# A graph attention and expert kernel on one core: TensorE runs a step's tail ends first, then tail weights, weighted sum and logits, and both folds together behind them

## What is computed

```python
x = x + L0_gnn(layernorm(x), adj, W, a)      # 8192 nodes, 256 features
x = x + L0_ffn(layernorm(x), ...)            # router over 32 experts, top 1

def L0_gnn(h, adj, W, a):
    Wh = h @ W
    e = (Wh @ a1)[:, None] + (Wh @ a2)[None, :]
    e = where(e > 0, e, 0.2 * e)
    e = where(adj > 0, e, -9e15)             # adj: 8192 x 8192 int32, about 4 ones in a row
    return elu(softmax(e, axis=1) @ Wh)

def L0_ffn(xf):
    idx = argmax(xf @ router_w.T + router_b)
    h = relu(xf @ W1[idx] + b1[idx])
    return relu(h @ W2[idx] + b2[idx])
```

## Time and profile before

| | before |
|---|---|
| time, median of 3 runs | 1303.84 us (1300.76 to 1303.9) |
| the profiled execution's own time | 1299.63 us |
| its span, from first to last instruction | 1297.9 us |
| busy: PE, DVE, ACT, POOL | 891.5, 886.2, 716.9, 669.2 us |
| mean granted TensorE clock | 0.834 of full |

### The profile page before, as it was taken

One profiled execution on the slowest core, in us unless ns is written; L12 is line 12 of the kernel. 1 busy time (PEld: TensorE's weight loads), 2 busy tenths in 40 slices (PEclk: granted clock), 3 DMA queues, 4 the chain that ended last, 5 costly groups with the idle time before them and its releaser, 6 DMA issues.

```text
span 1297.9 us, 24517 instructions
## 1 busy us (share of the span) xinstructions
PE 891.5 (69%) x3976; PEld 570.7 (44%) x4016; DVE 886.2 (68%) x4330; ACT 716.9 (55%) x1083; POOL 669.2 (52%) x700
## 2 busy tenths in 40 slices
PE   3777567777667777667667766777776766378784
PEld 2555334444444444444444444444443444265563
DVE  5877357777777777777777777776777765544443
ACT  1444556665666666566666566666566621055553
POOL 3555355555555555555555545565555556145553
PEclk9999878787877878877888877787878887589998
DMA  5778879888898888888888888898888894044442
GB/s 208 261 260 293 307 280 338 325 323 318 331 332 310 326 327 326 323 314 324 322 323 323 318 334 323 314 338 326 336 323 315 315 238 113 18 133 123 137 141 73
DMA packets 103146, 357.33 MB, mean 275 GB/s; under 512 B 28054, under 2 KB 54639, under 8 KB 70337
## 3 DMA queue, kind: packets, MB, share of 16 engines
q1 hardware_dynamic: 74658, 296.79, 64.0%
q0 software_dynamic: 27712, 60.06, 13.7%
q10 hardware_dynamic: 736, 0.05, 0.0%
HBM read 343.67 MB, written 32.05 MB: 289 GB/s over the span
## 4 chain that ended last, share of the span: by engine, by line
issue 24%; DVE 23%; PE 21%; DMA 11%; POOL 7%; SPq 5%; another core or an unknown queue 4%; DVEq 2%; ACT 1%; POOLq 0%; ACTq 0%
DMA G_all<-wh_table,idx 7%; PE psF L1456 7%; POOL G_all L571 5%; PE psO L1521 5%; SPq L471 3%; SPq L475 2%; PE psW L1445 2%; DVE top_word L844 2%; DMA regions<-x,posu 2%; DVE xn L1113 1%; PE psW L1491 1%; PE psW L1507 1%; DVE begun L1013 1%; DVE lidx L1128 1%
## 5 line engine op out<-in xcount | busy, mean ns | idle before, releaser
L675 ACT ACTIVATE sg<-raw_all,minus_half 128x2048 fp8e4<-128x2048 int32 x256 | 497.8, 1989 | 0.2 <-DMA raw_all<-in_adj 0.2
L571 POOL DMA_INDIRECT G_all<-wh_table,idx x384 | 411.7, 1072 | 137.7 <-issue 128.5
L1456 PE MATMUL psF<-sg,fold_w 128*128 128x512 fp8e4 x1024 | 334.6, 486 | 0.0
L593 POOL DMA_INDIRECT regions<-x,posu x64 | 67.4, 1053 | 312.9 <-DVE idx L1005 165.3
L689 ACT ACTIVATE hh<-psO,rden 128x256 f32<-128x256 f32 x64 | 30.3, 473 | 286.4 <-DVE xn L1113 286.0
L1521 PE MATMUL psO<-G_all,diag 128*128 128x256 f32 x640 | 176.0, 427 | 4.4 <-DVE diag L1070 2.3
L1456 PEld LDWEIGHTS psF<-sg,fold_w 128*128 128x128 fp8e4 x1024 | 114.3, 120 | 145.9 <-issue 93.8
L1521 PEld LDWEIGHTS psO<-G_all,diag 128*128 128x128 f32 x640 | 134.1, 220 | 23.2 <-issue 4.8
L1507 PE MATMUL psW<-slot_s,to_row 128*128 128x11 f32 x128 | 33.8, 340 | 136.3 <-DVE slot_s L1041 90.9
L632 POOL DMA_INDIRECT out_x<-yb,tok x81 | 79.0, 976 | 81.5 <-DVE yb L1393 44.1
L844 DVE MAX8 top_word<-psF 128x8 f32<-128x256 f32 x256 | 102.9, 424 | 14.2 <-remote 7.9
(11 more groups left out here) (213 smaller groups left out, 1771.6 us busy)
## 6 DMA issues: line engine op xcount, KB each, us to landing
raw_all<-in_adj SPq DMA_DIRECT2D x256, 1024.0 KB
xb<-regions SPq DMA_DIRECT2D x84, 130.0 KB
wh_table<-G_all POOLq DMA_DIRECT2D x8, 1040.0 KB, 10.2
x_sb<-in_x SPq DMA_DIRECT2D x8, 1024.0 KB, 5.7
G_all<-wh_table,idx POOLq DMA_INDIRECT x384
regions<-pad_row SPq DMA_DIRECT2D x32, 130.0 KB
x_sb<-in_L_ffn_W SPq DMA_DIRECT2D x4, 512.0 KB
x_sb<-in_L_ffn_W SPq DMA_DIRECT2D x8, 256.0 KB
```

Source lines behind the costliest of these rows:

```text
L571: pool.indirect_dma_start(out=G[par][:, k, :], out_offset=None, in_=table[:, :], in_offset=bass.IndirectOffsetOnAxis(ap=idx[par][:, k:k + ...
L593: pool.indirect_dma_start(out=region[:, :], out_offset=bass.IndirectOffsetOnAxis(ap=posu[par][:, 0:1], axis=0), in_=x1[par][:, :], in_offs ...
L675: act.activation(sg[par][:, q, :], raw[q], ACT.Sign, bias=minus_half[:, 0:1], saturate=False).then_inc(a_sg, 1)
L1456: pe.matmul(words, fold_w[:, j, :], sg[par][:, 2 * h:2 * h + 2, j * WORDS:(j + 1) * WORDS], start=(j == 0), stop=False)
```

## The change

Only the order in which TensorE issues a step's work is changed. `tail_ends(u + 2)` goes to the place behind `tail_scores`, ahead of `tail_weights`; `fold(u + LAG, par, 0)` goes from that place to just ahead of `fold(u + LAG, par, 1)`, behind the logits. No other engine's order is changed, and no instruction is added or removed.

```diff
             def step(u, par, do):
                 if do.attend:
                     tail_scores(u, par)
-                if do.search:
-                    fold(u + LAG, par, 0)
+                if do.prepare:
+                    tail_ends(u + 2)
                 if do.attend:
                     tail_weights(u, par)
                     weighted_sum(u, par)
                 if do.place:
                     logits(u - 2)
-                if do.prepare:
-                    tail_ends(u + 2)
                 if do.search:
+                    fold(u + LAG, par, 0)
                     fold(u + LAG, par, 1)
                 if do.prepare:
                     tail_slots(u + 2, par)
```

## The result

| | before | after |
|---|---|---|
| time, median | 1302.94 us (1300.76 to 1303.9, 4 runs) | 1420.76 us |
| ratio | | 1.0903, 95% interval 1.0877 to 1.0928 |
| the profiled execution, its span | 1299.63, 1297.9 us | 1419.34, 1417.6 us |
| mean granted TensorE clock | 0.834 | 0.822 |

The change costs 9.0%. Of four runs after (1417.16 to 1506.48 us; the median is of all four) the longest was disturbed and is left out of the ratio.

The account below looks back on a forecast made before the run. No engine's busy share bounds it; VectorE's queue is followed. Search +5.3 us, tail_row's wait -2.14, gather -0.11: step +3.0; 56 steps +168, four others +15, together +183 on 1299.6: 1482, as median 1486 us; range 1405 to 1560.

Parts of the forecast that it names:

- the forecast's own case: Whole kernel: a time of 1463 to 1514 us, given 68%.
- rival A: TensorE at full clock through the whole burst: step grows 0.6 to 1.0 us, total time 1340 to 1364 us; 7%.
- Tail ends first: TensorE's tail ends issued early: removes VectorE's wait in front of tail_row, 2.14 us a step, at no cost.
- Sum no longer behind fold 0: TensorE's weighted sum starts at about 573.5 in place of 574.11; worth 0.
- Fold 0 behind sum and logits: VectorE's quarter 0 search waits for sum, logits and fold 0: 5.14 us at full clock, 9.9 at half.
- The clock: TensorE cold when the sum begins, warm 5.1 us later (4.1 to 6.1); fold 0 ends at 581.1 (580.6 to 581.5).
- The rest: Fold 1, tail slots, ranks and late signals 0; the gather wait in front of slot_s goes, 0.11 us a step.
- B: TensorE at half clock through fold 0 as well: step +5.4 us, total time 1625 us; 6%.
- C: Not slower: tail_row's removed wait pays for fold 0's move; step stays 15.1 us, total time 1304 us; 2%.
- D: DMA stream, share 0.88, is the true pace and swallows the shift; total time 1304 us; 1%.
- the signs named ahead: Profile after: step 17.9 to 18.2 us, some 5 us wait at first search, DMA share near 0.74, span near 1480.
- the Trainium skill's rule on bursts: Back-to-back matmuls stay at full clock, giving a 5.14 us burst, not 7.6; prediction held the trace spoke against it.

Follow-up runs that it names:

- e2: Kernel before with only fold 0 moved behind logits and tail ends, tail ends not brought forward; 1397.95 us, ratio 1.1487 on a 1217 us chip.
- e6: Changed kernel plus sixteen matmuls a step on constants in TensorE's idle time, results unused; 1367.15 us, ratio 1.0489 to the kernel before, 1303 us chip.
- e3: Changed kernel with fold 0 done also at its old place, result unused; 1386.94 us, ratio 1.1389 to the kernel before on a 1217 us chip.
- e5: Changed kernel with VectorE's searches of quarters 0 and 1 moved behind xn2; 1386.3 us, ratio 1.0644 to the kernel before on the 1303 us chip.
- e9: Kernel before with SyncE issuing an adjacency quarter only when the last but one has landed; 1219.81 us, ratio 1.0025 on a 1217 us chip.

## Why the prediction was right, and where its terms were off

The mechanism was the forecast one: fold 0's end paces the step, and the sum in front of it pays for the cold clock. The time, 1420.8 us, lies 65 us under the 1486 of the forecast: inside the range of 1405 to 1560, but outside the forecast's own case (1463 to 1514, held to be 68% likely), in the stretch between it and rival A that had been given 6%. The added 118 us are less than two thirds of the forecast 183. Point by point:

1. *Tail ends first.* Their wait is gone, 2.14 us to 0, as forecast. That this brings nothing beside the late fold is the lesson of e2: without it the step is the same. In the sum of the prediction it was rightly a wait replaced by a longer one. The search now ends so late that the signal would be there anyway.

2. *Sum no longer behind fold 0.* Forecast to start 4.2 us behind slot_s; 609.66 - 605.47 = 4.19.

3. *Fold 0 behind sum and logits.* From the sum's start to the search I had 5.15 + 0.37 + 2.10 = 7.6 us; it took 6.91 (4.23 + 0.37 + 2.31). So the search moved by 4.6 us (6.48 to 11.10), not 5.3.

4. *The clock*, the mis-sized term. It was cold when the sum began, as forecast, but full 3.2 to 3.5 us later, not 5.1. Even the range of that term (4.1 to 6.1) was too late: I read it off bursts that began right behind tail_scores. Now the burst begins 3.7 us behind tail_scores (606.01 to 609.66), with the tail ends and weights between; counted from tail_scores the clock rises 6.8 and 7.3 us on. That it rises so much earlier after the sum's start is measured; why is not, and no run tells it. By e6 the full clock takes 1.6 us off the sum.

5. *The rest.* The forecast kept 2.14 + 0.11 us of the 5.3 back. The loss of the search, 4.6 us, shrinks to 17.07 - 15.05 = 2.0 a step, so 2.6 were given back: 2.14 by tail_row's wait, 0.13 by slot_s's (7.9 us / 53 to 1.2 / 53), and some 0.3 by waits too small to name one. 56 steps x 2.02 = 113 us of the 119.7 by which the span grew.

Step and total together: 3.0 forecast, 2.02 measured; 0.7 of the difference is the search (4: clock -0.9, fold to search +0.2), 0.3 the waits that went along.

The rivals: A (full clock, 1340 to 1364) fell by the clock; with the full clock put back, e6 came to 1367, next to its upper number, and with a held signal, as it had reckoned with; that it comes so near is in part luck, since e6's constant matmuls also delay the sum. B (half clock through fold 0) fell: fold 0's eight matmuls take 1.89 us. C (not slower) fell by the wait of 4.8 us. D (the DMA stream as the pace) fell: its share went to 0.77, where I had forecast 0.74. Of the signs named ahead, the wait of some 5 us (4.8), its releaser (L1458 for 123.0 of the 253.5 us, the rest remote), tail_row's 0, the sum's first instructions 0.43 us apart and the folds' spacing came; 17.9 to 18.2 us a step did not (17.07), nor the span of 1480 (1417.6).

The prediction held the Trainium skill's rule on bursts to be contradicted by the trace, and that was too quick. The Trainium skill ("TensorE: Matmul & The Clock Gate", "Loop structure matters more than you think") wants the next iteration's matmuls to follow at once, and gives a loop with a wait in each turn as the one that goes cold. Here some 8 us with nothing but small matmuls lie between fold 1 and the next sum (618.3 to 626.4). The denser burst did not keep the clock (0.80 in the looped stretch, 0.81 before), filling the pause between the bursts kept it for more of the time (0.90 in e6's looped steps), at a price: both agree with the Trainium skill.

## What to carry to other kernels

Before work is moved behind other work on an idle-looking engine, ask who consumes it and what stands behind that consumer in its queue: here a fold that ran for nothing in TensorE's free time came to hold up VectorE's search, and with it everything VectorE does later in the step. A wait that vanishes in such a profile may only be covered by a longer one; the part that seems to gain has to be run alone, and on more than one chip. Cold matmuls are cheapest where nobody waits for them: the early fold paid the cold start for the sum.

## What the runs showed of the hardware

- Three different kernels (the changed one, e2, e3), the last two on the other kind of chip, came to the same mean step, 17.06 to 17.07 us, with the same pattern of the granted clock: 6.8 us at 1.2 GHz, 10.2 at 2.4, and between 230 and 1000 us no stretch of another length in any of the three. Where a step's length hangs on when the clock rises, and the clock follows the step's load, the two seem to lock: a burst that begins earlier meets more of the slow stretch. That reading is argued; shown is only that e3's quite different burst gave the same step, and that the kernels whose clock followed another pattern (e6, e5) left it.
- The kernel before takes 1303 us on one kind of chip and 1217 us on the other. On the first kind VectorE stands 2.1 us a step in front of tail_row for a matmul that, in the step of the earlier trace rows, began 1.9 us before tail_row; on the second the nearest profile (e9) shows 0.4 us. On the first kind the wait ends behind one of SyncE's adjacency issues: of the 53 tail_rows of the earlier trace rows 46 wait longer than 1.5 us, and in each of the 46 the issue stands 0.08 to 0.30 us ahead of tail_row, 0.25 in the median. What holds the signal stays open: e9, which spaces these issues, was run only where the kernel before takes 1217 us, and changed nothing there (1.0025, interval 0.9985 to 1.0064). It isn't the whole difference of the chips either: some 25 us lie in the third phase, which reads no adjacency.
